# Second stage of a two-layer convolution kernel: the sum of nine tap products reaches the output by two adding stores instead of one

## The reference, cut to what matters

```python
# --- layer 0 ---
x = x + blur4x4(_gn(x))                       # (16, 512, 64, 64), depthwise 4x4 blur
# --- layer 1, on v = _gn(x) ---
t   = relu(group_norm(d4_1x1(v, w1)))         # 256 channels
wgt = einsum('oi,bighw->boghw', w2, t) + b2   # 9 tap weights for each of 4 groups, 8 rotations, pixel
xv  = d4_1x1(v, w_v)                          # 512 channels of values
pats = unfold_patches(xv, 3)                  # the 9 shifted copies of the values
x = x + (wv * pats).sum(axis=4)               # wv: wgt, its 3x3 taps turned for each rotation
```

## Time and profile before

| | us |
|---|---|
| median of 3 runs | 5064.24 (5059.03 to 5066.26) |
| the profiled execution | 5067.52 |
| its span, first to last instruction | 5065.8 |
| first stage in that span | 0 to about 1140 |
| last period in that span | about 4819 to 5065.8 |

### The profile page before, as it was taken

One profiled execution on the slowest core, in us unless ns is written; L12 is line 12 of the kernel. 1 busy time (PEld: TensorE's weight loads), 2 busy tenths in 40 slices (PEclk: granted clock), 3 DMA queues, 4 the chain that ended last, 5 costly groups with the idle time before them and its releaser, 6 DMA issues.

```text
span 5065.8 us, 115951 instructions
## 1 busy us (share of the span) xinstructions
PE 4251.4 (84%) x38012; PEld 1455.9 (29%) x38012; DVE 4474.8 (88%) x7761; ACT 2860.6 (56%) x4642; POOL 4133.2 (82%) x2208
## 2 busy tenths in 40 slices
PE   8999999978988788888878787878787878788864
PEld 3333333322322222222222222222222222222221
DVE  6777777753999999999999999999999999999998
ACT  7999999966545444444545454545454544445421
POOL 6888888842989888888888888889898988798898
PEclk9999999989999999999999999999899999899976
DMA  8999999953545454444444454445454545444433
GB/s 237 256 258 256 258 256 258 256 133 88 126 94 117 93 117 101 105 103 104 113 97 113 97 122 93 113 103 116 94 125 93 116 92 116 97 113 101 96 75 65
DMA packets 872958, 679.47 MB, mean 134 GB/s; under 512 B 560224, under 2 KB 822752, under 8 KB 856032
## 3 DMA queue, kind: packets, MB, share of 16 engines
q1 hardware_dynamic: 835552, 538.55, 37.5%
q0 software_dynamic: 36864, 134.23, 17.2%
HBM read 404.21 MB, written 402.65 MB: 159 GB/s over the span
## 4 chain that ended last, share of the span: by engine, by line
POOL 44%; issue 13%; DVE 11%; PE 8%; POOLq 1%; ACT 1%; DVEq 0%; DMA 0%; SPq 0%; ACTq 0%
POOL acc L1046 43%; DVE prod_d L1098 3%; DVE prod_p L1098 2%; PE ps L783 2%; PE ps L770 2%; DVE ps L1142 2%; PE ps L793 1%; PE ps L742 1%; DVE ps L1098 1%; PE ps L732 1%; DVE six_t L1063 1%; DVE acc L1146 1%; POOL out L1035 1%; DVE x_bias L1090 1%; POOLq L1043 0%
## 5 line engine op out<-in xcount | busy, mean ns | idle before, releaser
L1046 POOL TENSOR_TENSOR acc<-acc,prod_p 128x1024 f32<-128x1024 f32 x1280 | 3093.1, 2417 | 302.9 <-DVE acc L1146 155.9
L1098 DVE TENSOR_TENSOR prod_p<-ps,val 128x1024 f32<-128x1024 f32 x1280 | 1558.6, 1218 | 128.8 <-POOL acc L1046 121.1
L793 PE MATMUL ps<-prod_d,base 128*128 128x512 f32 x1024 | 633.5, 703 | 583.8 <-DVE prod_d L1098 572.7
L1098 DVE TENSOR_TENSOR prod_d<-ps,val 128x512 f32<-128x512 f32 x1536 | 1041.5, 681 | 2.4 <-ACT ps L947 2.4
L300 PE MATMUL ps<-xn,band 64*64 64x512 f32 x8192 | 948.2, 598 | 21.5 <-issue 13.0
L742 PE MATMUL ps<-xh,wh 128*32 128x512 f32 x6144 | 765.8, 630 | 33.3 <-ACT t L906 21.9
L332 POOL TENSOR_TENSOR x_out<-x_out,x_in 128x512 f32<-128x512 f32 x512 | 636.4, 1275 | 0.0
L260 ACT ACTIVATE x_out<-ps 64x512 f32<-64x512 f32 x1024 | 606.3, 592 | 50.6 <-PE ps L300 29.2
L941 ACT ACTIVATE val<-ps 128x512 f32<-128x512 f32 (+1 forms) x640 | 356.3, 557 | 461.4 <-PE ps L770 453.8
L783 PE MATMUL ps<-t,w 128*32 128x256 f32 x9216 | 574.4, 401 | 40.2 <-DVE prod_d L1098 35.1
L770 PE MATMUL ps<-xm,base 128*32 128x256 f32 (+1 forms) x8192 | 589.3, 425 | 15.9 <-ACT xm L921 15.7
(11 more groups left out here) (75 smaller groups left out, 3393.6 us busy)
## 6 DMA issues: line engine op xcount, KB each, us to landing
x_in<-x SPq DMA_DIRECT2D x128, 1024.0 KB, 7.4
x<-x_out SPq DMA_DIRECT2D x256, 512.0 KB, 5.1
xr<-x SPq DMA_DIRECT2D x512, 256.0 KB, 3.5
out<-x SPq DMA_DIRECT2D x1024, 128.0 KB, 2.7
out<-acc POOLq DMA_DIRECT2D x256, 512.0 KB, 5.6
prod_p<-wsrc SPq DMA_DIRECT2D x1, 384.0 KB, 4.6
w<-w2t SPq DMA_DIRECT2D x1, 288.0 KB, 4.4
shift_m<-shifts SPq DMA_DIRECT2D x1, 256.0 KB, 5.6
```

The lines of the kernel that those rows point to most:

```text
L793: nc.tensor.matmul(ps[:, D_BANK, :], same, prod_d[:, 0, :], start=False, stop=True, skip_group_check=True)\
L1046: nc.gpsimd.tensor_tensor(acc[:, r, :], acc[:, r, :], prod_p[:, k % P_RING, :], ALU.add).then_inc(p_added, 1)
L1098: return nc.vector.tensor_tensor(dst.rearrange("p (m r w) -> p m r w", m=count, w=W), taps_of(tap).rearrange("p (m r w) -> p m r w", m=1, ...
```

## The change

Two things leave each other: VectorE's own sum in `acc` and GpSimd's sum of the pooled products.

- Pooled product 0 is written by VectorE into a new buffer `sum_p` (ring of 2) and not into `prod_p`. GpSimd adds products 1 to 4 to it in place: four adds in a granule, the first of which no longer waits for `own`.
- `acc` goes to the output by itself (`store_own`, issued after GpSimd's add of product 2), and `sum_p` by a second adding store (`store_sum`, issued after the first add of the next granule). The second waits for the landing of the first.
- `ACC_RING` falls from 4 to 2. VectorE waits for the landing of `store_own` two granules back before L1146 of a first half, and for the landing of `store_sum` two granules back before it writes product 0. SyncE's copies wait for `sum_stored` in the place of `stored`.

```diff
-ACC_RING = 4
+ACC_RING, SUM_RING, COPY_RING = 2, 2, 4
+NADD = NP - 1
+OWN_AT, SUM_AT = 2, 1
...
+    sum_p = sb("sum_p", [P, SUM_RING, QM * UPX])
...
-            if not first(i, n - ACC_RING + 1):
-                wait_apart(sp, sp_apart, stored[r], i * (16 * N_GRAN // ACC_RING) + 16 * (n // ACC_RING))
+            if not first(i, n - COPY_RING + 1):
+                wait_apart(sp, sp_apart, sum_stored[r % SUM_RING],
+                           i * (16 * N_GRAN // SUM_RING) + 16 * ((n - COPY_RING) // SUM_RING + 1))
...
-        def store(i, n):
-            r = n % ACC_RING
-            pool.wait_ge(p_added, i * (NP * N_GRAN) + NP * (n + 1))
-            pool.wait_ge(resid_in[r], i * (64 * N_GRAN // ACC_RING) + 64 * (n // ACC_RING + 1))
-            nc.gpsimd.dma_start(out[i, n], acc[:, r, :], accum_op=ALU.add).then_inc(stored[r], 16)
+        def store_own(i, n):
+
+            r, c = n % ACC_RING, n % COPY_RING
+            pool.wait_ge(own, i * (OWN * N_GRAN) + OWN * (n + 1))
+            wait_apart(pool, pool_apart, copied[c], i * (64 * N_GRAN // COPY_RING) + 64 * (n // COPY_RING + 1))
+            nc.gpsimd.dma_start(out[i, n], acc[:, r, :], accum_op=ALU.add).then_inc(own_stored[r], 16)
+
+        def store_sum(i, n):
+
+            img, at = (i, n) if n >= 0 else (i - 1, n + N_GRAN)
+            r = at % SUM_RING
+            pool.wait_ge(p_added, i * (NADD * N_GRAN) + NADD * (n + 1))
+            wait_apart(pool, pool_apart, own_stored[at % ACC_RING], i * (16 * N_GRAN // ACC_RING) + 16 * (n // ACC_RING + 1))
+            nc.gpsimd.dma_start(out[img, at], sum_p[:, r, :], accum_op=ALU.add).then_inc(sum_stored[r], 16)
...
-                r = n % ACC_RING
-                pool.wait_ge(own, i * (OWN * N_GRAN) + OWN * (n + 1))
-                for j in range(NP):
-                    k = NP * n + j
-                    pool.wait_ge(p_ready, i * (NP * N_GRAN) + k + 1)
+                total = sum_p[:, n % SUM_RING, :]
+                for j in range(1, NP):
+                    k = NADD * n + j - 1
+                    pool.wait_ge(p_ready, i * (NP * N_GRAN) + NP * n + j + 1)
                     if not first(i, k):
-                        pool.wait_ge(p_added, i * (NP * N_GRAN) + k)
-                    nc.gpsimd.tensor_tensor(acc[:, r, :], acc[:, r, :], prod_p[:, k % P_RING, :], ALU.add).then_inc(p_added, 1)
+                        pool.wait_ge(p_added, i * (NADD * N_GRAN) + k)
+                    nc.gpsimd.tensor_tensor(total, total, prod_p[:, k % P_RING, :], ALU.add).then_inc(p_added, 1)
+                    if j == SUM_AT and not first(i, n):
+                        store_sum(i, n - 1)
+                    if j == OWN_AT:
+                        store_own(i, n)
                     if more and (n, j) == RSTD_AT:
                         t_rstd_of(i + 1)
-                store(i, n)
...
+        store_sum(B - 1, N_GRAN - 1)
...
+            if j == 0:
+                dst = sum_p[:, n % SUM_RING, :]
+                if not first(i, n - SUM_RING + 1):
+                    dve.wait_ge(sum_stored[n % SUM_RING], i * (16 * N_GRAN // SUM_RING) + 16 * (n // SUM_RING))
+            else:
+                k = NADD * n + j - 1
+                dst = prod_p[:, k % P_RING, :]
+                if not first(i, k - P_RING + 1):
+                    dve.wait_ge(p_added, i * (NADD * N_GRAN) + k - P_RING + 1)
...
-                dve.wait_ge(stored[r], i * (16 * N_GRAN // ACC_RING) + 16 * (n // ACC_RING))
+                dve.wait_ge(own_stored[r], i * (16 * N_GRAN // ACC_RING) + 16 * (n // ACC_RING))
```

More of the change, by code:

```diff
@@ L509, in stage_b @@
     w_chain, w_built = sem("w_chain"), sem("w_built")
-    sp_apart, act_apart, dve_apart = (sem(f"b_{e}_apart") for e in ("sp", "act", "dve"))
+    sp_apart, act_apart, dve_apart, pool_apart = (sem(f"b_{e}_apart") for e in ("sp", "act", "dve", "pool"))
     setup = sem("b_setup")
@@ L524, in stage_b @@
     pe_added = sem("pe_added")
-    resid_in = [sem(f"resid_in{r}") for r in range(ACC_RING)]
-    stored = [sem(f"stored{r}") for r in range(ACC_RING)]
+    copied = [sem(f"copied{r}") for r in range(COPY_RING)]
+    own_stored = [sem(f"own_stored{r}") for r in range(ACC_RING)]
+    sum_stored = [sem(f"sum_stored{r}") for r in range(SUM_RING)]
     t_chain = sem("t_chain")
@@ L656, in copy_resid @@
         def copy_resid(i, n):
-            u, q4, r = (n // GRANS) % UNITS, n % GRANS, n % ACC_RING
-            if not first(i, n - ACC_RING + 1):
-                wait_apart(sp, sp_apart, stored[r], i * (16 * N_GRAN // ACC_RING) + 16 * (n // ACC_RING))
+            u, q4, r = (n // GRANS) % UNITS, n % GRANS, n % COPY_RING
+            if not first(i, n - COPY_RING + 1):
+                wait_apart(sp, sp_apart, sum_stored[r % SUM_RING],
+                           i * (16 * N_GRAN // SUM_RING) + 16 * ((n - COPY_RING) // SUM_RING + 1))
             img, at = i + n // N_GRAN, n % N_GRAN
@@ L665, in copy_resid @@
                 dst = out[img, at, 32 * q:32 * q + 32].rearrange("p (m n) -> p m n", m=QM)
-                sp.dma_start(dst, src).then_inc(resid_in[r], 16)
+                sp.dma_start(dst, src).then_inc(copied[r], 16)
         sp.dma_start(base[:], basis[:, 0:4 * P]).then_inc(base_in, 16)
@@ L695, in _ @@
         period(B - 1, more=False, ahead=False)
+        for r in range(COPY_RING):
+            sp.wait_ge(copied[r], 64 * B * N_GRAN // COPY_RING)
         for r in range(ACC_RING):
-            sp.wait_ge(resid_in[r], 64 * B * N_GRAN // ACC_RING)
-            sp.wait_ge(stored[r], 16 * B * N_GRAN // ACC_RING)
+            sp.wait_ge(own_stored[r], 16 * B * N_GRAN // ACC_RING)
+        for r in range(SUM_RING):
+            sp.wait_ge(sum_stored[r], 16 * B * N_GRAN // SUM_RING)
     @block.tensor
@@ L1108, in pooled @@
         def pooled(i, n, j):
-            k = NP * n + j
             if j in (0, 2, 4):
                 tap_wait(i, n, banks_of(P_TAPS[j]))
-            if not first(i, k - P_RING + 1):
-                dve.wait_ge(p_added, i * (NP * N_GRAN) + k - P_RING + 1)
-            product(n, P_TAPS[j], prod_p[:, k % P_RING, :], n % GRANS * QM, QM).then_inc(p_ready, 1)
+            if j == 0:
[7 more added lines that the diff above has]
+                    dve.wait_ge(p_added, i * (NADD * N_GRAN) + k - P_RING + 1)
+            product(n, P_TAPS[j], dst, n % GRANS * QM, QM).then_inc(p_ready, 1)
         def banks_of(tap):
```

## The result

| | before | after |
|---|---|---|
| median, us | 5063.1 (5059.03 to 5066.26, 4 runs) | 4974.4 (4966.6 to 4979.7, 4 runs) |
| ratio to before | | 0.9824, interval 0.9807 to 0.9841 |
| the profiled execution / its span | 5067.52 / 5065.8 | 4970.58 / 4968.9 |
| one period | 240.5 | 234.5, (4728.7 - 1211.7) / 15 |

The kernel became 1.8% faster. The forecast was 4966 us, within 4936 to 5016. The total is right; some of its terms are not, and the errors cancel.

A forecast was written before the change was run, and what follows sets the result against it. VectorE and GpSimd were taken to bound the kernel by turns. 5065.8 - 121.1 + 13.5 - 3.0 + 12 = 4967.2 us of span, 4968.9 for the run; with the profiled run 3.3 above the median, 4966 us, range 4936 to 5016.

The forecast's parts named there:

- Part 1: GpSimd's granule with four adds and two stores: 11.7 to 12.9 us, 12.3 taken, below VectorE's 13.21.
- the rival "nothing": GpSimd stays the pace because a store costs it 2.0 us, granule 14.1 us: 5054 to 5074 us, chance 0.06.
- Part 2, -121.1 us: All of VectorE's waits for GpSimd over the whole kernel go, as GpSimd becomes faster than VectorE: -121.1 us.
- a full ring: VectorE stopped because the buffers of pooled products were full, GpSimd being 0.84 us slower in a plain granule.
- Part 2, +13.5 us: At 15 borders between periods, 0.9 of 4.29 us comes back as VectorE's waits for tap biases: +13.5 us.
- the 29.8 us stay: VectorE's waits for TensorE in the second stage, 29.8 us, were expected to remain unchanged.
- TensorE's own chain, which moves along: TensorE's later waits at the border, 1.04 us and its like, depend on TensorE's own sequence, which shifts earlier too.
- Part 3, -3.0 us: At the kernel's end the last store is issued 4.8 us earlier, less 1.76 already counted: net -3.0 us.
- Part 4a, +12 us: VectorE's product 0 waits for a store's landing, 0.8 us a period: +12 us, between 0 and 130.
- (b) to (e): New waits of both stores, VectorE's L1146 and SP's copies: 0 each, the copies at most 1 us a period.
- Landings did not crowd: Rival: landings at 7.4 us make VectorE wait in plain granules, 69 us in place of 12: 5023 us, chance 0.20.
- The slower one: Rival: store landings of 8.4 us set the pace, plain granules 14.6 us: 5189 us, chance 0.06.

## Why the prediction was right, and where it was not

- **Part 1, GpSimd's granule.** Right: no idle time before a store whose waits are old, 0.3 us more on the add behind it (2.69 against 2.39). With five adds and two stores 13.84 us were measured; one add of 2.53 less is 11.3, just below the range of 11.7 to 12.9. This also puts the rival "nothing" away.
- **Part 2, -121.1 us.** The step that failed. It read every idle time with GpSimd's name as a full ring. The 3.20 us of the earlier trace rows are VectorE's loop turn: gone when the loop is written out, there with an empty ring. In the trace of before such stands, 2.8 to 4.0 us, come 13 times, once in each turn, 40.5 us together; the next longest is 1.76 us. That was the clue. What the runs showed in its place: of the 128.8 us before these products, 88.3 were thus GpSimd's and all went; of the turns 37.5 us stay.
- **Part 2, +13.5 us, and "the 29.8 us stay".** The border did give back, but not by the tap bias: over the whole kernel the waits for TensorE grew by 18.3 us, behind TensorE's own turn and its lower clock. Both were there before (a mean idle time of 2.7 us, and 4.25 us for the 48 matmuls), and the prediction had not seen them. "TensorE's own chain, which moves along" holds for the chain, not for the turn, which grew by 0.5 us.
- **Part 3, -3.0 us.** The right direction, -1.7 measured by the same reading (16.4 to 14.7 us from the last product to the end).
- **Part 4a, +12 us.** 14.3 measured in 20 waits of at most 1.2 us; the landing's median is 5.5 us, though its queue's share doubled from 17.2% to 34.5%. (b) to (e) cost nothing that the table of waits shows.
- **Not in the sum:** the small operations (-20.8 us) and the rest of the table, by the estimate there the overlap lost at each stop (-15.7 us). These two, 36.5 us, made up for the 29.8 us too many in part 2 (121.1 for 91.3), the 4.8 us that the waits for TensorE grew beyond the 13.5, and 3.6 us of landing and end. The direction and the main cause, GpSimd's pace, were foreseen; that the total came out within 10 us was luck.
- **The rivals.** Landings did not crowd. The slower one did not come, and one place later in GpSimd's order it would have: 5145 us.

## To carry to other kernels

A stand at the head of a hardware loop's body may be the turn of the loop, whatever releaser the trace names; compare it with stands of the same line elsewhere. Take the turns away engine by engine: here only the one on the chain to the next period's first inputs paid. When an edit gains nothing, look whether its time went into the next wait at the same place: by their ratios the small operations and the landing were worth nothing here one at a time and TensorE's loop 33 us, and all together, with VectorE's loop, 142 (0.9824 to 0.9543).

## What the runs showed of the hardware

- At the turn of a hardware loop over the periods VectorE stood 2.4 to 4.5 us and TensorE 2.2 to 6.3, and loads of instructions come with it; the short loop of the first stage turned in 0.21 to 0.25 us on TensorE, without a load. The cost on TensorE is not fixed (means of 2.6 to 5.2 us between kernels; within one kernel branches of 3.5 to 6.3 us, the three longest where the last adding store was issued 1.0 to 1.7 us before).
- A stand of 2.4 us on TensorE was followed by a granted clock of 0.56, and 48 matmuls took 3.90 us; behind a stand of 1.7 us the clock was 1.00 and they took 2.80.
- VectorE operations of 128x2 with two inputs in SBUF took up to 3.0 us beside GpSimd's adds, 0.16 us with one input in PSUM.
- An adding store of 512 KB landed in 5.5 to 6.0 us (medians) with one or two stores in a granule; two issued one behind the other put the second at 8.7 us (store one add later, the median of `out<-acc`). The estimate of 3.2 us by the Trainium skill (DMA: Bandwidth & Descriptors, Anatomy of one DMA) was too short in every run.
- A store issued by GpSimd costs it about 0.6 us and a slower add behind it, and 0.61 to 0.76 us more when its wait is for the add just ahead.
